# Memory attention of a perceiver block: one more memory unit drained by VectorE, and the output projection placed behind the seventh unit

## What is computed

```
    mem = _split_heads(memories @ Wm)
    k = jnp.concatenate([k, mem], axis=2)
    v = jnp.concatenate([v, mem], axis=2)
    dots = jnp.einsum('bhid,bhjd->bhij', q, k) * scale
    attn = jax.nn.softmax(dots, axis=-1)
    out = jnp.einsum('bhij,bhjd->bhid', attn, v)
    out = out.transpose(0, 2, 1, 3).reshape(b, n, h * d)
    return out @ Wo + bo
```

## Time and profile before

| | us |
|---|---|
| median of 3 runs | 2050.87 (2049.24 to 2051.6) |
| the profiled execution | 2051.98 |
| its span in the trace | 2050.2 |
| TensorE busy | 1970.7 (96%) |
| VectorE busy | 1237.9 (60%) |
| ScalarE busy | 874.4 (43%) |

### The profile page before, as it was taken

The page is one execution under the profiler, slowest core; times in us unless marked ns, Lnnn a source line. Parts: engine busy times, 40 slices in busy tenths (PEclk is TensorE's granted clock), DMA queues, the critical chain, the costliest instruction groups (busy, mean ns, idle before and its releaser), DMA issues. The chain is left out here.

```text
span 2050.2 us, 34616 instructions
## 1 busy us (share of the span) xinstructions
PE 1970.7 (96%) x14134; PEld 1429.1 (70%) x14134; DVE 1237.9 (60%) x2088; ACT 874.4 (43%) x2059; POOL 118.9 (6%) x134
## 2 busy tenths in 40 slices
PE   7999999899999999999999999999999999989999
PEld 6864455578878888854445788777777777774677
DVE  6456489463355888899999511265454454548553
ACT  4224443253333333489997432233232332333342
POOL 0000000000000000110000000011101010100122
PEclk9999999999999999999999999999999999999999
DMA  7210000121110110120002235477577584743001
GB/s 269 75 58 1 1 2 3 43 98 52 41 43 21 42 62 21 62 82 21 21 1 83 65 123 148 140 202 194 149 199 197 147 215 126 201 141 98 1 0 42
DMA packets 124573, 178.93 MB, mean 87 GB/s; under 512 B 12144, under 2 KB 81264, under 8 KB 123952
## 3 DMA queue, kind: packets, MB, share of 16 engines
q1 hardware_dynamic: 114336, 162.03, 26.4%
q10 hardware_dynamic: 10080, 14.68, 2.7%
HBM read 124.91 MB, written 29.75 MB: 75 GB/s over the span
## 5 line engine op out<-in xcount | busy, mean ns | idle before, releaser
L1584 ACT ACTIVATE R<-R 128x64 f32<-128x64 f32 x896 | 217.0, 342 | 3.4 <-DVE R L2309 3.4
L1315 ACT ACTIVATE R<-bank 128x512 f32<-128x512 f32 (+1 forms) x134 | 79.8, 599 | 323.4 <-PE bank L973 224.4
L970 PE MATMUL bank<-cth,wmh 128*128 128x512 f32 x512 | 207.2, 405 | 5.3 <-ACT arena L1689 3.3
L970 PE MATMUL bank<-cth,wml 128*128 128x512 f32 x512 | 200.3, 391 | 0.0
L540 PE MATMUL bank<-XN,arena 128*128 128x512 f32 x320 | 147.2, 612 | 0.0
L973 PE MATMUL bank<-ctl,wmh 128*128 128x512 f32 x512 | 137.3, 390 | 0.0
L970 PEld LDWEIGHTS bank<-cth,wmh 128*128 128x128 f32 x512 | 96.1, 188 | 35.7 <-issue 14.3
L540 PE MATMUL bank<-Y,arena 128*128 128x512 f32 x256 | 116.4, 600 | 1.7 <-ACT H L1627 1.7
L1689 ACT ACTIVATE arena<-bank,small 128x289 f32<-128x289 f32 x128 | 62.9, 501 | 126.5 <-issue 125.2
L540 PEld LDWEIGHTS bank<-XN,arena 128*128 128x128 f32 x320 | 60.9, 196 | 71.1 <-issue 70.7
L973 PEld LDWEIGHTS bank<-ctl,wmh 128*128 128x128 f32 x512 | 96.1, 188 | 20.6
(11 more groups left out here) (442 smaller groups left out, 4242.4 us busy)
## 6 DMA issues: line engine op xcount, KB each, us to landing
Y<-value_turn SPq DMA_DIRECT2D x168, 128.0 KB, 3.1
H<-in_ctxT SPq DMA_DIRECT2D x30, 512.0 KB, 5.1
arena<-in_L_attn_mlp_w SPq DMA_DIRECT2D x8, 1024.0 KB, 5.3
probs<-R SPq DMA_DIRECT2D x14, 512.0 KB, 2.9
probs<-R ACTq DMA_DIRECT2D x14, 512.0 KB, 4.9
R<-probs SPq DMA_DIRECT2D x56, 128.0 KB, 4.0
R<-probs ACTq DMA_DIRECT2D x56, 128.0 KB, 4.7
R<-value_rows SPq DMA_DIRECT2D x32, 132.0 KB
```

The source lines that it names most:

```text
L970: mm(bank, w_[:, o // 4, k, tl(o % 4)], cth[:, k, :, :], start=(k == 0 and w_ is wmh), stop=False)
L1315: fn(dst, src, ACT.Copy).then_inc(act_bank_free, 1)
L1584: last = fn(into[:, x // 2, h, :, x % 2], RC["Ey"][:, t, h, :], ACT.Copy, scale=RC["Ex"][:, t, h, 8 * j + x:8 * j + x + 1])
```

## The change

`BY_DVE` also holds unit 5, so that four of the eight units are drained by VectorE and four by ScalarE. In the pair loop TensorE does unit 5 right behind unit 4, after the second scores. Unit 6 now follows `out_rows`, and the output projection of pairs 4, 8 and 12 stands behind it. VectorE copies unit 5 after it has transposed the second batch's probabilities. ScalarE writes the second batch's probabilities out before it copies unit 0, and issues the loads that read them back before it copies unit 1. Everything that waited for unit 4 to be drained by VectorE now waits for unit 5 as well or instead.

```diff
-BY_DVE = (2, 3, 4)
+BY_DVE = (2, 3, 4, 5)
...
+                on_dve(("mem", pr, 5))
                 on_dve(("mem", pr, 4))
...
-                fill(4)
+                fill(4, 5)
                 fill(0, 1)
                 if pr:
                     out_rows(pr - 1)
+                if at_edge(pr):
+                    prob_blocks(b0)
+                    prob_blocks(b1)
+                fill(6)
                 if pr and pr % (CB // 2) == 0:
                     on_act(("ot", pr - 1))
                     output(pr // (CB // 2) - 1)
-                if at_edge(pr):
-                    prob_blocks(b0)
-                fill(5)
-                if at_edge(pr):
-                    prob_blocks(b1)
-                fill(6)
...
-            memory(0, (0, 1, 5, 6))
+            memory(0, (0, 1, 6))
...
                 exponentials(b1)
-                fill(0)
                 if not at_edge(pr):
                     act.wait_ge(probs_turned[1], 2 * pr)
...
-                fill(1)
-                if pr:
-                    out_rows(pr - 1)
-                fill(5)
+                fill(0)
                 if not at_edge(pr):
                     act.wait_ge(probs_spilled[1], 16 * pr)
...
+                fill(1)
+                if pr:
+                    out_rows(pr - 1)
                 fill(6, 7)
...
                 on_act(("mem", pr, OT1 - 1))
+                stored(("mem", pr, 5))
                 stored(("mem", pr, 4))
...
-            memory(1)
+            memory(1, (2, 3, 5))
...
                     turn_probs(b1)
+                    memory(pr + 1, (5,))
...
-            sp.wait_ge(dve_bank_full, UV.at[("mem", PAIRS - 1, 4)] + 1)
+            sp.wait_ge(dve_bank_full, UV.at[("mem", PAIRS - 1, 5)] + 1)
```

## The result

The changed kernel takes 2053.47 us in the median of 17 runs (2046.03 to 2057.57), the kernel before, beside it, 2050.1 (2047.26 to 2053.07). The ratio is 1.0016, with a 95% interval of 1.0008 to 1.0023. So the change gains nothing that can be measured; my forecast of 2046.0, 0.24% faster, was wrong.

A forecast was written before the change was run, and what follows sets the result against it. A ring of bank copies was taken to set the 29.96 us round. Removing 6.7 + 0.7 + 2.6 and giving back 4.0 + 1.2 left 4.9 us (unrounded) off the median 2050.87: 2046.0, range 2042.5 to 2051.0.

The forecast's parts named there:

- The bank ring: Pair loop: copies, splits, VectorE's transposes and ScalarE's exponentials freeing a bank set 29.96 us rounds; moving unit 5 removes 6.7 us.
- the value wait: TensorE's time from tail transpose to first weighted sum above 3.27 us, summed over fourteen pairs; forecast to grow from 5.1 to 9.0.
- The value ring: Tail, splits, VectorE's transposes, SyncE's write and reads, value moves, next pair's first weighted sum: not shortened, 4.0 us given back.
- ScalarE's earlier loads: Probability loads issued 0.8 us earlier, nearer SyncE's value moves: 0.25 us for each ring, 1.2 us given back in all.
- my upper bound of 0.8: ScalarE's loads, issued 0.8 us earlier, stand wholly in front of the value moves; gain then 2.2 us in sum.
- The sign that I had taken for the rival: Ordinary pairs whose loads came soonest behind the value moves were also those whose moves landed latest, 5.0 to 5.7 us.
- The output projection: Pairs 4, 8 and 12: placed behind unit 6, which covers ScalarE's `out_rows` copy; 2.6 us removed.
- ScalarE standing at its write: Output pairs: ScalarE waits for its probabilities to be written, 26.2 to 26.7 us after the previous tail, before loads and copies.
- Nothing elsewhere: Outside the ordinary pairs: pairs 0 and 15 keep their order, unit 5 ahead of the loop has spare banks; no cost.
- The short stalls: TensorE's stops without a named releaser within runs of small products, 7.7 us in all, carried over unchanged.
- The rival that half of them go: Longer waits ahead of small products hide half of TensorE's unnamed stops: 3 to 4 us more gained, 2042.5; chance 0.12.
- The value ring keeps most of it: ScalarE's loads push the value moves by 0.4 to 1.2 us; gain 4.1 down to 0.2, about 2048.5; chance 0.36.

## Why the prediction was wrong, point by point

**The bank ring: right.** Units 4, 5 and 0 follow without a wait, no unit waits for the exponentials any more, and ordinary rounds of 29.96 became 28.9 to 32.4. The two kernels with a late write and unit 5 at its old place show the ring by itself: the value wait gone, the round unmoved.

**The value ring: the place was right, its size and its cause were not.** I forecast that the value waits would grow from 5.1 to 9.0, and with the loads to 10.3. They are 10.0, 13.4 and 11.3; in pair 9 alone 2.2, 2.4 and 2.7 (forecast 2.5 to 3), in pair 13 only 1.9, 1.0 and 1.0. But I took the ring as something that only the loads could touch. 2.6 us of its 33.2 came from one DMA of ScalarE's that ran beside SyncE's loads: with it late the waits are 0.1 to 1.9 in all seven profiles. The waits that I booked as the price of the faster loop were the price of the write's place, which the kernel before pays too, with 5.2 us.

**ScalarE's earlier loads: a step that failed.** I charged 0.25 us a ring, from an even share of the DMA engines. The landing rose by 0.73, 0.89 and 0.51 us (mean 0.7), near my upper bound of 0.8. All of the rise lies behind the issue: SyncE is through with issuing the moves 28.5 to 28.6 us after the tail in the kernel before and in all three profiles of the changed one. With the loads alone put late, the moves land 4.7 us after their issue instead of 5.4, which shows the loads as the cause. The sign that I had taken for the rival, moves landing latest where the loads came soonest, doesn't hold over the trace: in pair 14 the loads began 1.5 us behind the first move and the last landed 6.1 us after its issue, in pair 3 it was 1.1 and 4.2. By my own bounds a push of 0.7 would cost some 3.5 us (an estimate between 1.2 at 0.25 and 4.0 at 0.8), so this step alone would still have left a gain of 2.6.

**ScalarE's write: charged with nothing, and not part of the miss, but the lost gain.** The change moves the write past unit 0's copy, yet it starts 21.8 us after the tail before and after, so it adds nothing to the difference between the two kernels. Left behind the copy, it would have gone 2.2 us later together with unit 0, and the value wait would have fallen instead of rising to 10 to 13 us: it is 0.2 to 0.8 in the variants with all of ScalarE's DMAs late, and 9.1 where only the loads are. The experiments with the write alone show that it weighs more than the loads: it doubles the time that SyncE needs to issue its four loads. The rule of the Trainium skill that I weighed, from "DMA: Bandwidth & Descriptors", "Issuing engines are not separate DMA queues", says that several issuing engines save only issue time; the traces here show the issue time itself getting longer, 3.4 us against 1.8.

**The output projection: right** in place (it follows unit 6 without a gap) and near in size: 3.4 us of the loop alone, 2.6 forecast. What I said of ScalarE standing at its write held too; without unit 6 as cover it cost 20 us.

**"Nothing elsewhere": the other step that failed.** From the last tail to the end the changed kernel takes 259.2, 260.1 and 259.6 us, before 257.4. Its last pair is longer by 4.4, 4.9 and 5.0 us (22.0 to 22.6 from its tail transpose to the next, against 17.6), by two stops in its scores and, in two of the three profiles, half clock behind the first. 2.3 to 2.9 us of that come back, because the last weighted sum stops for 1.1 to 1.4 us and not for 3.71, and half clock behind it lasts 6.8 us and not 10.2. So the stops did not appear from nothing: they moved, with the count of products, to other places of the program. I had the row of one such stop, and the 3.71 as the longest in the earlier trace rows, and carried them over "unchanged", without asking where in the program they stand.

**The short stalls: right in the loop.** The rival that half of them go didn't come true: the idle times without a releaser within the small products of the loop, the value wait left out, are 5.3 us before and 5.6, 5.3 and 5.3 in the changed kernel (counting those of over 0.15 us; my 7.7 was counted from starts).

**The account.** Mean of the three profiles: loop 463.4, so 1.8 gained; behind it 2.2 lost; together 0.4 slower, where the three ratios have a mean of 1.0002. Against the forecast of 4.9 faster that is 5.3 short: 1.3 from longer value waits (11.6 against 10.3), 2.3 from half-clock stretches in the loop (0, 1.7 and 5.1, estimates as above), 2.2 from behind the loop. That is 0.5 more than is missing. The 2.3 stand in the profiles, but the clock means of the runs don't confirm them; that term stays open. The first set, the one that the forecast is measured by, was slower than the two others by 0.2%. Its runs had a lower mean clock than theirs (0.9874 against 0.9882 and 0.9877), which can be a part of it; the rest stays open too.

**The rivals.** "The value ring keeps most of it" is what happened in the loop, at the push of 0.4 to 1.2 us that it names; but it ends at a gain of 0.2, and the rest of the way to 2053.47 came from elsewhere. The range ended at 2051.0: it left no room for a loss by stops and clock. I had the stops only as a gain and the clock not at all.

## What to carry to other kernels

When a step moves on an engine that also issues DMAs, cost each DMA in it, the writes too, by what another queue is issuing at that moment, and not only by the bytes. Work out when the step will start in time, since its place in the list of instructions can change while its time stays. A wait that looks like the length of a ring may be one badly placed transfer: look at how long the issue of the neighbouring DMAs takes, and try the transfer later before taking the ring as given. And compare stretches of the trace and several runs: a single profile here stood 6 us ahead for reasons that lay a thousand us in front of the change.

## What the runs showed of the hardware

- **Issue time depends on the other queue.** Four loads of 128 KB took SyncE 1.8 us to issue, and 3.4 us while a write of 512 KB that ScalarE had issued ran. Starting that write 2.5 us later shifted the last value moves' issue by 1.6 us and their landing by 2.6.
- **TensorE stops at fixed places of its program, until its instructions have come.** Runs of small products stop without a semaphore, for up to 3.7 us; counted from the last tail transpose, kernels of one order stop before the same products. All 103 such stops of over 0.6 us end 1.2 to 1.7 us after a packet of 16 KB on the DMA queue of the kind "instruction" has arrived. That the stops are longer while other DMAs are busy is likely and not shown throughout: with the next stage's weights held back one stop went, another that now met the weights grew from 0.92 to 3.60 us, and a third, ahead of them in both kernels, grew from 0.67 to 2.21.
- **Half the clock behind some short stops.** 1.94 us without products among small ones was followed by 3.4 us at 0.50, and the unit in it took 4.42 us instead of 2.85; waits of 5 us in front of the projection came with 6.8 us at 0.50, and the projection took 1.9 to 2.8 us longer. It doesn't follow every such stop: behind one of 1.92 us, at 1656.9 in the first profile of the variant with late DMAs, the clock stayed in full.
